# One fused attention and feed-forward layer on one core: the reciprocals' transposes moved behind the maxima's, GpSimd's and the other queues reordered, some copies given to ScalarE

## The reference

```python
x = x + xattn(layernorm(x), ctx, Wq, Wkv, Wout)       # 16 heads of 16, softmax over 64 keys, causal mask
x = x + ffn(layernorm(x), w1, g1, w2, g2, w3, g3)     # hidden width 1024

def ffn(x):
    h = silu(linear(x, w1, g1)) * linear(x, w2, g2)
    return linear(h, w3, g3)

def linear(x, w, g):
    xn = g * x / sqrt(mean(x * x) + 1e-8)
    s = 127 / clip(max(abs(xn)), 1e-4)                # per token
    xq = clip(round(xn * s), -128, 127) / s
    a = mean(abs(w))
    wq = round(tanh(w / (a + 1e-8))) * arctanh(a)     # -1, 0 or 1 times one number
    return xq @ wq.T
```

## Time and profile before

| | |
|---|---|
| median of 3 runs | 221.17 us (220.50 to 221.46) |
| the profiled execution | 221.68 us, its span 219.8 us |
| mean granted TensorE clock | 0.898 of full speed |
| busy share of the span | PE 76%, DVE 70%, ACT 65%, POOL 56% |
| instructions | 3409 |

### The profile page before, as it was taken

The page is one execution under the profiler, slowest core; times in us unless marked ns, Lnnn a source line. Parts: engine busy times, 40 slices in busy tenths (PEclk is TensorE's granted clock), DMA queues, the critical chain, the costliest instruction groups (busy, mean ns, idle before and its releaser), DMA issues.

```text
span 219.8 us, 3409 instructions
## 1 busy us (share of the span) xinstructions
PE 166.9 (76%) x1114; PEld 113.1 (51%) x1114; DVE 154.8 (70%) x297; ACT 143.2 (65%) x193; POOL 122.5 (56%) x230
## 2 busy tenths in 40 slices
PE   8699679794895796696593993896666998998543
PEld 7177556563763664554562663362334464645332
DVE  0328253984689785775894896089698999999982
ACT  2033557861763865855882968658979998989740
POOL 8142807137054237238256183327789999999950
PEclk9769799999589679679999797589999999999999
DMA  7999910000000000000000000000000010100102
GB/s 145 319 378 368 374 65 0 0 4 1 0 1 0 3 0 0 0 3 0 0 1 0 3 0 0 0 3 0 0 25 25 27 48 28 48 24 24 51 24 72
DMA packets 9216, 11.35 MB, mean 52 GB/s; under 512 B 1584, under 2 KB 7984, under 8 KB 9200
## 3 DMA queue, kind: packets, MB, share of 16 engines
q1 hardware_dynamic: 8656, 10.62, 14.6%
q10 hardware_dynamic: 544, 0.52, 1.3%
HBM read 9.04 MB, written 2.10 MB: 51 GB/s over the span
## 4 chain that ended last, share of the span: by engine, by line
issue 21%; PE 21%; POOL 19%; DVE 18%; ACT 17%; DMA 3%; SPq 1%; POOLq 0%; DVEq 0%; ACTq 0%
ACT q_x L785 6%; PE bank L475 6%; POOL half_sum L337 5%; PE bank L492 4%; DVE row_sum L926 3%; POOL w_in L425 3%; DMA ctxT<-in_ctxT 3%; DVE u L958 2%; ACT probsT L745 2%; PE wide L511 2%; ACT wT L771 2%; PE wide L595 2%; POOL m_h L435 2%; ACT recipT L757 2%; POOL fb_a L346 2%
## 5 line engine op out<-in xcount | busy, mean ns | idle before, releaser
L425 POOL TENSOR_TENSOR w_in<-hh,g3b 128x1024 f32<-128x1024 f32 x15 | 35.4, 2360 | 1.1 <-DVE hh L1095 1.1
L660 PE MATMUL wide<-wT,xqT 128*128 128x512 bf16 x128 | 31.4, 388 | 2.2 <-DVE hh L1095 2.2
L475 PE MATMUL bank<-ident,probs 128*128 128x128 f32 x128 | 23.0, 339 | 8.6 <-ACT probsT L745 8.6
L327 POOL TENSOR_SCALAR ln_ve<-ln_mv 128x2 f32<-128x2 f32 x8 | 1.8, 227 | 46.8 <-DVE ln_mv L894 46.8
L684 PE MATMUL bank<-wT,hT 128*128 128x256 bf16 x128 | 16.7, 274 | 10.9 <-DVE hT L1122 10.0
L475 PEld LDWEIGHTS bank<-ident,probs 128*128 128x128 f32 x128 | 19.0, 176 | 11.5 <-issue 11.2
L745 ACT COPY probsT<-bank 128x512 f32<-128x512 f32 x32 | 17.6, 587 | 9.7 <-PE bank L475 9.7
L854 ACT ACTIVATE q_h<-w_in,round_c,qs_h 128x1024 f32<-128x1024 f32 x16 | 19.9, 1241 | 5.9 <-DVE qs_h L1116 5.9
L765 ACT ACTIVATE probs<-wide,ln_rstd 128x1024 f32<-128x1024 f32 x16 | 17.0, 1112 | 8.8 <-PE wide L527 8.8
L337 POOL TENSOR_TENSOR half_sum<-probs 128x512 f32<-128x512 f32 x16 | 21.9, 1389 | 0.8 <-ACT probs L765 0.8
L926 DVE TENSOR_REDUCE row_sum<-half_sum 128x32 f32<-128x1024 f32 x8 | 9.7, 1218 | 17.7 <-POOL half_sum L337 17.7
(11 more groups left out here) (138 smaller groups left out, 360.7 us busy)
## 6 DMA issues: line engine op xcount, KB each, us to landing
out<-y SPq DMA_DIRECT2D x16, 128.0 KB, 1.7
w_in<-in_w1T SPq DMA_DIRECT2D x1, 1024.0 KB, 7.9
w_in<-in_w2T SPq DMA_DIRECT2D x1, 1024.0 KB, 11.8
w_in<-in_w3T SPq DMA_DIRECT2D x1, 1024.0 KB, 13.0
xT<-in_xT SPq DMA_DIRECT2D x1, 1024.0 KB, 9.4
x_sb<-in_x SPq DMA_DIRECT2D x1, 1024.0 KB, 11.9
x_sb<-in_x SPq DMA_DIRECT2D x2, 256.0 KB, 5.7
xT<-in_xT SPq DMA_DIRECT2D x1, 512.0 KB, 8.7
```

What stands on the lines that cost most here:

```text
L425: g.tensor_tensor(out=c_h[:, t, :], in0=hh[:, t, :], in1=g3b[:], op=ALU.mult).then_inc(c_ready, 1)
L475: return nc.tensor.matmul(out, in_, ident[0:n, 0:n], is_transpose=True, start=True, stop=True)
L660: last = nc.tensor.matmul(wide[:, (w * 2 + n) * 512:(w * 2 + n + 1) * 512], xqT[:, T, w * DC + c, :], wT[:, cols:cols + 512], start=(c == ...
```

## The change

It reorders all four queues and adds three things: a second buffer for u, a warming exponential behind the Ln, and copies of odd tiles' transposed bits by ScalarE instead of VectorE. The core of the diff, by engine:

```diff
 # transfers
-                for n in range(2):
-                    sp.dma_start(ctxT[:, :, n, :], ctxT_d.rearrange("l (b k) -> l b k", k=SK)).then_inc(ctx_ld, 16)
+                sp.dma_start(ctxT[:].rearrange("l b n k -> l (b n k)"), ctxT_d).then_inc(ctx_ld, 16)
...
 # GpSimd, iteration(j)
                         keys(j + 2)
-                        norm(j + 2)
                     if j >= 1:
-                        factor(j - 1)
-                    if j >= 1 and live(j + 1):
...
                         values(j + 1)
-                    if live(j + 1):
-                        half_sums(j + 1)
+                        factor(j - 1)
+                    if j == B - 2:
+                        pool.wait_ge(w_down_ready, 1)
+                        product_scales(0, 4)
+                    half_sums(j + 1)
+                    if live(j + 2):
+                        norm(j + 2)
                     if j >= 1:
                         token_scales(j - 1)
...
-                pool.wait_ge(w_down_ready, 1)
-                product_scales(0, 6)
+                product_scales(4, 2)
...
 # TensorE, maxima_T(b): another bank, so another wait
-                    need(pe, rT_ready, b)
+                    need(pe, qT_ready, b + 1)
...
 # TensorE, ahead of the ring
                 last.then_inc(mean_done, 1)
+                keep_warm(4)
...
-                for oc in range(DC):
-                    query(1, oc)
+                query(1, 0)
                 pe.wait_ge(sel_ready, 1)
                 maxima_T(0)
                 pe.wait_ge(v_early, 1)
                 values_of(4)
                 subtract_maxima(0)
+                query(1, 1)
...
 # TensorE, iteration(j)
+                    scores(j + 1)
                     if j == 0:
                         pe.wait_ge(v_late, 2)
-                    if live(j + 1):
-                        scores(j + 1)
-                    if j > 0:
-                        recip_T(j)
...
                     probs_T(j, 0)
                     probs_T(j, 1)
-                    if j == 0:
-                        recip_T(j)
                     maxima_T(j + 1)
+                    recip_T(j)
+                    subtract_maxima(j + 1)
                     if live(j + 2):
                         query(j + 2, 0)
-                    subtract_maxima(j + 1)
                     weigh(j)
...
 # ScalarE, ahead of the ring and iteration(j)
                 values_copy(6)
+                abs_sums(1)
...
-                    if j > 0:
-                        recip_widen(j)
+                    recip_widen(j)
                     if j >= 2:
                         quantise(j - 2)
-                    if j > 0:
-                        recip_T_copy(j)
                     probs_T_copy(j, 0)
-                    if j == 0:
-                        recip_widen(j)
                     probs_T_copy(j, 1)
-                    if j == 0:
-                        recip_T_copy(j)
+                    recip_T_copy(j)
                     exponentials(j + 1)
...
                         a.activation(w_ln[:], w_ln[:], ACT.Ln).then_inc(ln_out, 1)
+                        a.activation(warm_exp[:], round_c[:, 1:2], ACT.Exp)
...
 # ScalarE, a new step, and the loop over T (T runs to NT + 1 now)
+                def hidden_T_copy(T, t):
+                    need(act, hT_done, T + 1)
+                    need(act, down_done, T - 1)
+                    a.copy(hT[:, t, :, :].rearrange("p n k -> p (n k)").bitcast(fp32),
+                           hT_banks[t][:]).then_inc(hT_ready[t], 1)
...
+                    if live_tile(T - 2) and t == 1:
+                        hidden_T_copy(T - 2, t)
+                    if T == 1:
+                        tokens_T_copy(5)
-                    if T == 2:
+                    if T == 3:
                         quantise(6)
-                    if T == 3:
+                    if T == 5:
                         tokens_T_copy(6)
-                    if T == 4:
                         quantise(7)
-                    if T == 5:
+                    if T == 7:
                         tokens_T_copy(7)
...
 # VectorE, iteration(j)
+                    if j == 6:
+                        log_branch()
                     maximum(j + 1, 0)
...
+                        aggregate_sum(j - 1)
                     maxima_T_copy(j + 1)
+                    if j >= 1:
+                        centre_gain(j - 1)
...
                     divide(j)
+                    if 3 <= j < 6:
+                        ternary(j - 3)
                     if j >= 1:
                         token_max(j - 1)
-                    if 3 <= j < 6:
-                        ternary(j - 3)
+                    sums(j + 1)
                     if j == 1:
                         weight_means()
                     if j == 2:
                         series()
+                    if j == 3:
                         log_input()
-                    if j == 6:
-                        log_branch()
-                    sums(j + 1)
```

More of the change, by code:

```diff
@@ L48, in build_program @@
     L = ctxT_d.shape[0]
-    SK = ctxT_d.shape[1] // B
+    SK = ctxT_d.shape[1] // (2 * B)
     H = w1T_d.shape[1]
@@ L160, in build_program @@
         y = sb("y", [P, 2, D])
+        warm_exp = sb("warm_exp", [P, 1])
         wide = bank("wide", 2048)
@@ L714, in _ @@
                         up(T + 1, 1)
+                    if T == 0:
+                        project(7)
                     if live_tile(T + 2):
                         up(T + 2, 0)
+                    if T == 1:
+                        column_sums()
                     if live_tile(T - 2):
@@ L784, in quantise @@
                         for w in range(2):
-                            last = a.activation(q_x[:, t, w, :], u[:, t, w, :], ACT.Identity,
+                            last = a.activation(q_x[:, t, w, :], u[:, b % 2, t, w, :], ACT.Identity,
                                                 scale=qs_x[:, b, t, w:w + 1], bias=round_c[:, 0:1])
@@ L861, in _ @@
                 recip_T_copy(7)
+                square(0, 0, 0)
                 silu(1, 1, 0)
                 quantise(5)
-                tokens_T_copy(5)
-                for T in range(NT + 1):
+                for T in range(NT + 2):
                     t = T % TB
@@ L1150, in _ @@
                         gated(T, t)
+                    if T == 1:
+                        residual(7)
+                        measure_sum(7)
                     if last_tile(T):
```

86 lines of the change are left out of this document (39 added, 47 removed).

## The result

| | before | after |
|---|---|---|
| median (lowest to highest) of 4 runs | 220.83 us (219.79 to 221.46) | 195.99 us (194.81 to 197.18) |
| ratio, 95% interval | | 0.8879 (0.8814 to 0.8944) |
| profiled execution | 221.68 us | 195.91 us |
| granted clock | 0.898 | 0.947 |
| busy share PE, DVE, ACT, POOL | 76, 70, 65, 56% | 82, 77, 76, 66% |

What follows compares the result with a forecast made beforehand. It took waits around the attention cycles, where no engine is full, and GpSimd at the end as bounds. 221.68 - 4.1 (A) - 10.7 (B) - 3.7 (C) - 0.6 (D) = 202.6 us; range 196 to 211.

Steps and rivals of the forecast that it cites:

- the ring: The six attention cycles from batch 1's exponentials to batch 7's, 92.57 us before, with no engine full.
- rival 1: Whole kernel: the clock stays up throughout, giving 199.2 us; chance 0.25.
- B: The six attention cycles: earlier half sums and shorter waits, 81.85 against 92.57 us, so -10.7; bounds -14.1 and -2.6.
- Exp to widening: In each attention cycle, exponentials' start to ScalarE's widening of the reciprocals: 5.6 us without the ternary pass, 7.85 with it.
- The falls: Attention cycles: TensorE's clock drops in the two cycles of 14.3 us, costing +1.7 us each.
- The first move: Attention cycles: reciprocals' transposes and copy placed behind the maxima's transposes, directly saving 0.47 us a cycle.
- A: Start up to batch 1's exponentials: full clock for first products, fewer waits, -4.1 us; -0.5 if the clock falls.
- C: Batch 7's exponentials to GpSimd's g3 product of tile 14: earlier first tile, partly taken back by ScalarE, -3.7 us.
- Rival 3: First feed-forward tiles: ScalarE, with the added copies, bounds them and takes all of C, giving 206.3 us; chance 0.12.
- D: Tail behind GpSimd's last g3 product: VectorE drops one copy, -0.6 us, bound 0.
- Rival 2: Attention cycles: the stop ahead of the second transposes drops the clock in five, 2.3 us each: 210.7 us; chance 0.15.
- Rival 4: Attention cycles: TensorE never leaves the 1.2 GHz level; with four such cycles 230.4 us; chance 0.03.

Runs made afterwards that it cites:

- e9: Changed kernel with only the next tokens' scales put back ahead of the half sums on GpSimd: 211.34 us.
- e8: Changed kernel with products of ones that nothing reads added where TensorE waited: 192.09 us, ratio 0.8708 to the kernel before.
- e12: Changed kernel with the context brought by two transfers again, the four warming products kept: 195.37 us.
- e7: Changed kernel with TensorE's old transition order: batch 5's tokens, last projection and column sums ahead of the loop over the tiles: 201.39 us.
- e5: Changed kernel without the four warming products, the context's single transfer kept: 196.48 us.
- e6: Changed kernel with VectorE copying the FFN's bits of all tiles, as before: 196.62 us.
- e2: Changed kernel with the reciprocals' transposes and ScalarE's copy of them back ahead of the probabilities' for batches 1 to 6: 195.45 us.
- e10: e8 with the reciprocals' transposes and ScalarE's copy of them back ahead of the probabilities' for batches 1 to 6: 193.25 us.
- e4: Kernel before with the reciprocals' transposes and copies behind the maxima's, maxima in their new bank, subtraction ahead of the half query: 218.09 us.
- e11: e8 with the row sums and their reciprocals ahead of the token maxima on VectorE: 198.41 us.
- e3: Kernel before with GpSimd's new order inside the batch loop alone: 207.74 us.

## Why the prediction was right, and where it was off

The sign, the ring as the main place, and the mechanism held; the time came out 6.6 us under the forecast, at the lower edge of the range, and even under rival 1, which had no fall of the clock, though two came. Step by step:

**B was mis-sized**, by 6.0 us of the 6.6. The mechanism is the one the prediction read in the earlier trace rows: half sums held behind a wait of 7.15 us; e9 shows that putting this wait back alone costs 15 us. Two parts of its sum were too large.
- *Exp to widening.* The six came out at 5.44, 5.83, 6.34, 7.56, 7.51 and 7.56, together 40.2; the prediction had 44.25 (78.45 less six times 5.7). It was right on the plain cycle (5.6) and near on the ternary pass, which is held by the second half sum as foretold (2.17 in place of 1.42). The tanh did hold the third widening (6.34, right behind it), less than the 7.0 foretold. But the prediction also added every tiny VectorE operation and the series to the cycle. The weights' steps stand behind the row sums in VectorE's queue; they delayed no widening.
- *The falls.* Two cycles lost the clock, the two foretold, but against e8 a fall cost 1.34 in the fourth cycle and 0.45 in the sixth, not 1.7 in each. That it was those two is luck: with the same ring, e12 lost the fourth and fifth, e7 the third to fifth, e5 and e6 the third to sixth, and a cycle with a fall was at most 1.4 longer than in e8.
- *Widening to exp* was 5.6 as a mean in e8 (33.86 for six), near the prediction's 5.7, but partly by luck. Of the cycles with a quantisation it is 5.31 in the fifth, which has no weights' step on VectorE, and 5.65 to 6.21 in the four that have some. Here they count: in e8's sixth cycle they stand ahead of the maxima on VectorE, for which TensorE then waits 0.44. The prediction had them besides its 5.7.

**The first move** stood in the sum with 0.47 a cycle. Measured for batches 1 to 6: 0.15 to 0.2 a cycle with the clock up, 0 in the changed kernel (e2, e10). The prediction saw that the stop would move and lengthen, but didn't weigh the lengthening against the move.

**A was right**, in both halves. The first scores came 3.7 earlier (12.27 against 15.97), as foretold, and exp 0 1.4 later against them (forecast 1.7), so exp 0 came 2.3 earlier (forecast 2.0); from there to exp 1 it took 2.5 less (forecast 2.1, the two waits taken away). That the warming holds the clock, as the sum had it, is borne out by e12. It is not alone in that: without it the keys' products keep theirs behind the earlier landing, and the query loses it (e5). And the start of before can run at full clock by itself (e4), so the first half is a gain in some executions only.

**C was right**: 14.26 and 59.17, foretold 15.3 and 59.2. Within it, e7 puts 7.0 on TensorE's order at gain 1 where 4.8 had been charged, which leaves 1.2 for the rest where 2.4 had been; with a fall of the clock in e7's 7.0 this split is rough. That the odd tiles' copies on ScalarE earn nothing in the loop is shown by e6. Rival 3, that ScalarE takes all of C, falls with C itself: 3.5 of the 8.2 won at gain 1 were taken back.

**D had the wrong sign** in the changed kernel: +0.5 where -0.6 had been forecast, for want of a clock fall in the sum. With the clock held, e8 has -0.6, against a tail of before that had kept its clock too (0.99 from gain 14 on). That the dropped copy gives this 0.6 is not shown by itself, since e6's tail had a fall. The prediction had looked for falls in the ring only.

Rival 1 (no falls) is e8: in the ring it gains 1.7 on the changed kernel, where 3.4 had been given it, and the rest of its 3.9 lies outside. Rival 2 would have needed five cycles with a fall at 2.3 each; two had one here, four in e5 and e6, and each cost less. Rival 4 did not come: no cycle runs at the lower clock throughout.

On the price of a table switch the trace decided as the sum had it. ScalarE's timeline after, in the sixth cycle:

```profile
95.69 1.28 ACT L827 ACT_TABLE_LOAD   x1
96.98 0.20 ACT L827 ACTIVATE w_ln<-w_ln 128x3 f32<-128x3 f32 x1
97.21 1.28 ACT L829 ACT_TABLE_LOAD   x1
98.50 0.20 ACT L829 ACTIVATE warm_exp<-round_c 128x1 f32<-128x1 f32 x1
```

Each load is followed by the next activation within 0.01 us. The page "ScalarE: Activation LUTs" of the Trainium skill, section "What ACT_TABLE_LOAD costs", gives 2.66 us for a switch; these two show 1.3 each.

That the ternary pass is stretched only while a half sum runs fits what the page "SBUF — State Buffer" of the Trainium skill says in its section "SBUF: two separate sides": GpSimd and some VectorE operations take a shared port in turn, and the one that starts second is blocked. Here the pass took 2.17 and ended 1.09 behind the half sums. In e7's sixth cycle it started ahead of the second half sum instead: it took 1.22, and the two half sums 3.59 in place of 2.51.

## What to carry to other kernels

In an in-order queue, look for the instruction that waits for something needed late and stands ahead of something needed now: putting that one step back cost 15 us here, and the move that gave the change its title was worth 2.5 in the first cycle, with the maxima's new bank, and at most 1.2 in the six others. When an edit shortens a queue by joining two stops of TensorE into one, count the clock too; products of ones in the stops made the kernel 3.9 us shorter, 2.8 of it in the ring and the tail. When two chains of nearly equal length meet, advancing one at the cost of the other can lose more than it wins: in e11 1.7 us were won ahead of the widenings and 5.9 lost behind them.

## What the runs showed of the hardware

- The clock can fall while TensorE is busy, behind an idle that seemed to have passed: in e5 the keys' products behind 1.07 of waiting ran at full rate (2.02, granted clock 0.95), and the query right after them at half (3.56, 0.54).
- The same idle does not always end alike: 2.36 at 89.02 passed in the changed kernel and 3.35 at 210.98 in the kernel before, while 0.79 at 186.82 in the changed kernel, with 1.70, 1.66 and 1.21 in the nine us before it, was followed by a granted clock of 0.68 and then 0.62. And the same start, in e3 and e4, ran at half and at full rate.
- Products that nothing reads cost next to nothing where TensorE waits anyway: six in the ring took 1.50 us out of a stop of 2.4 to 3.1, and TensorE's busy time rose from 64.06 to 68.03 in cycles that became 1.7 shorter. The three cycles that got them and had no fall to lose, the second, third and fifth, became 0.02 to 0.04 longer.
